# A pairwise-interaction kernel on one core: two straight blocks become turned ones, and VectorE sums three slots of a block instead of four

## The reference, cut to what matters

```
e = stack([tbl_f[ids[:, f]] for f in 0..31], axis=1)   # 1024 x 32 x 64, float32
p, q = e[:, ROW_IDX], e[:, COL_IDX]                    # the 496 pairs of 32 fields
z = einsum('bne,hne,bnh->bn', p, kernel, q)            # 1024 x 496
h = concatenate([z, dense_ctx], axis=1)                # 1024 x 512
h = maximum(h @ W_top1 + b_top1, 0)                    # 512
h = maximum(h @ W_top2 + b_top2, 0)                    # 256
y = h @ W_top3                                         # 1
```

## Time and profile before

| what | us |
|---|---|
| median of 3 runs | 391.44 (390.27 to 391.60) |
| the profiled execution, device time | 391.53 |
| its span in the profile | 389.6 |
| PE, PEld, DVE, ACT, POOL busy in it | 362.7, 281.7, 349.3, 330.6, 241.8 |

### The profile page before, as it was taken

The page is one execution under the profiler, slowest core; times in us unless marked ns, Lnnn a source line. Parts: engine busy times, 40 slices in busy tenths (PEclk is TensorE's granted clock), DMA queues, the critical chain, the costliest instruction groups (busy, mean ns, idle before and its releaser), DMA issues.

```text
span 389.6 us, 13484 instructions
## 1 busy us (share of the span) xinstructions
PE 362.7 (93%) x4800; PEld 281.7 (72%) x4800; DVE 349.3 (90%) x449; ACT 330.6 (85%) x2889; POOL 241.8 (62%) x260
## 2 busy tenths in 40 slices
PE   0467999999999999999999999999999999999996
PEld 0254757689677976799678976799668976789666
DVE  0248999999999999999999999999999999999981
ACT  1037789789998999989998999989998999989992
POOL 5677777767765776667765776767766676740000
PEclk9968899999999999999999999999999999999999
DMA  3565881111111111111111111111111111110000
GB/s 82 174 197 182 248 287 30 29 26 28 27 26 25 26 27 27 26 25 26 30 25 26 24 29 27 29 25 26 30 25 25 25 29 25 26 23 2 3 3 2
DMA packets 14563, 19.27 MB, mean 49 GB/s; under 512 B 7192, under 2 KB 7840, under 8 KB 14496
## 3 DMA queue, kind: packets, MB, share of 16 engines
q0 software_dynamic: 8192, 8.40, 10.9%
q1 hardware_dynamic: 6304, 10.00, 8.0%
HBM read 18.39 MB, written 0.00 MB: 47 GB/s over the span
## 4 chain that ended last, share of the span: by engine, by line
PE 82%; POOL 4%; ACT 4%; DMA 3%; DVE 3%; issue 3%
PE u_ps L618 28%; PE u_ps L625 26%; PE side_ps L639 13%; PE side_ps L674 5%; PE acc_ps L674 5%; POOL emb L380 4%; ACT prod_s L429 4%; DMA emb<-tbl,ids_sb 3%; PE u_ps L601 2%; DVE prod_s L534 2%; PE u_ps L705 1%; PE side_ps L698 1%; PE side_ps L666 1%; DVE prod_t L517 1%; DMA ids_sb<-ids 0%
## 5 line engine op out<-in xcount | busy, mean ns | idle before, releaser
L429 ACT ACTIVATE prod_s<-prod_s 128x64 f32<-128x64 f32 x1405 | 307.2, 327 | 43.2 <-DVE prod_s L534 43.1
L380 POOL DMA_INDIRECT emb<-tbl,ids_sb x256 | 241.6, 944 | 106.7 <-issue 44.2
L429 ACT ACTIVATION_READ_ACCUMULATOR prod_s<-prod_s 128x1 f32 x1405 | 269.2, 253 | 0.0
L534 DVE TENSOR_TENSOR prod_s<-u_ps,emb 128x1024 f32<-128x1024 f32 (+4 forms) x224 | 150.2, 718 | 10.7 <-PE u_ps L625 10.0
L517 DVE TENSOR_TENSOR prod_t<-u_ps,emb_t 128x1024 f32<-128x1024 f32 x128 | 152.8, 1213 | 4.7 <-PE u_ps L618 4.7
L618 PEld LDWEIGHTS u_ps<-emb_t,k_sb 64*128 64x128 f32 x2048 | 134.4, 192 | 21.6 <-issue 7.9
L618 PE MATMUL u_ps<-emb_t,k_sb 64*128 64x128 f32 x2048 | 140.3, 280 | 3.7 <-DVE emb_t L506 2.4
L625 PE MATMUL u_ps<-k_sb,emb_t 64*128 64x512 f32 (+5 forms) x704 | 131.5, 484 | 1.1 <-DVE emb_t L506 0.8
L625 PEld LDWEIGHTS u_ps<-k_sb,emb_t 64*128 64x128 f32 x704 | 62.8, 193 | 22.7 <-DVE prod_s L534 8.3
L639 PE MATMUL side_ps<-prod_t,pick_sb 128*32 128x256 f32 x1024 | 63.3, 382 | 0.1
L639 PEld LDWEIGHTS side_ps<-prod_t,pick_sb 128*32 128x32 f32 x1024 | 32.0, 109 | 21.4 <-issue 3.5
(11 more groups left out here) (27 smaller groups left out, 43.1 us busy)
## 6 DMA issues: line engine op xcount, KB each, us to landing
k_sb<-k_pairs SPq DMA_DIRECT2D x9, 512.0 KB, 3.7
emb<-tbl,ids_sb POOLq DMA_INDIRECT x256, 2.4
k_sb<-k_pairs SPq DMA_DIRECT2D x6, 480.0 KB, 4.5
w_sb<-w SPq DMA_DIRECT2D x1, 1024.0 KB
w_sb<-w SPq DMA_DIRECT2D x1, 512.0 KB
k_sb<-k_pairs SPq DMA_DIRECT2D x1, 448.0 KB, 4.3
h<-dense SPq DMA_DIRECT2D x8, 8.0 KB, 2.1
out<-y_row SPq DMA_DIRECT2D x8, 0.5 KB
```

The source lines that it names most:

```text
L380: nc.gpsimd.indirect_dma_start(emb[t % EMBS][:, f * EMBED:(f + 1) * EMBED], None, tables[f], bass.IndirectOffsetOnAxis(ap=ids_sb[:, t, f:f ...
L429: done = nc.scalar.activation(slot, slot, ACT.Copy, accum_out=to[:, column:column + 1])
L534: done = nc.vector.tensor_tensor(product[:, :, cols], u[:, :, cols], low, ALU.mult)
```

## The change

Blocks 6 and 23 become turned (18 turned, 14 straight). Two turned chunks have room for 16 blocks only, so the sums of the last two turned blocks go to chunk 2, 8 rows of each of its 32-row quarters; the other 24 rows of each quarter come from h0. VectorE sums 3 slots of each straight block, in 7 pairs. ScalarE's sums fall from 176 to 166 a tile. The portions of picks are 4, 4, 5 and 5 blocks, in place of four times 4, and the first portion comes after n = 22. The core of the diff:

```diff
-    order = "SSTTTSSSTSTTTSST" "TSTTSTSSSTTSSTST"
+    order = "SSTTTSTSTSTTTSST" "TSTTSTSTSTTSSTST"
-ON_DVE = 4
+ON_DVE = 3
+IN_CHUNKS = T_CHUNKS * P // (HALVES * SLOTS)      # 16
+EXTRA = NT - IN_CHUNKS                            # 2
+GAP = EXTRA * HALVES * 2                          # 8
+SHARED = QUAD - GAP                               # 24
 def sum_place(b, half, d):
-    return d % T_CHUNKS, QUAD * (half * HALVES + d // T_CHUNKS), b
+    if b < IN_CHUNKS:
+        return d % T_CHUNKS, QUAD * (half * HALVES + d // T_CHUNKS), b
+    return T_CHUNKS, QUAD * d, (b - IN_CHUNKS) * HALVES + half
-PORTIONS = 4
-PORTION = NT // PORTIONS
-LATE_SPREAD_AT, SUMS_AT, LATE_SUMS_AT, SPREAD_AT = 4, 23, 27, 31
+PORTION_AT = [0, 4, 8, 13, 18]
+PORTIONS = len(PORTION_AT) - 1
+LATE_SPREAD_AT, SUMS_AT, LATE_SUMS_AT, SPREAD_AT = 4, 22, 27, 31
 ...
+            for sums in h0:
+                nc.vector.memset(sums[:, :P].rearrange("p (q r) -> p q r", q=QUADS)[:, :, :GAP], 0.0)
 ... pick_sums, for a block past the sixteenth:
+                            for d in range(LOW):
+                                chunk, quad, place = sum_place(b, half, d)
+                                cols = slice(half * BANK + d * P, half * BANK + (d + 1) * P)
+                                done = nc.tensor.matmul(
+                                    side_ps[quad:quad + QUAD, chunk],
+                                    pick_sb[:, 30 - 2 * place:62 - 2 * place], prod_t[at % TRING][:, cols],
+                                    start=(b == IN_CHUNKS and half == 0), stop=False)
 ...
             def late_spread(t):
-                pick_sums(t, 3 * PORTION, NT)
-                spread_straight(t, side_ps[:, T_CHUNKS:]).then_inc(side_spread, 1)
+                pick_sums(t, 3)
+                spread_shared(t)
+                spread_row(t, side_ps[:, CHUNKS - 1]).then_inc(side_spread, 1)
+            def spread_shared(t):
                 pe.wait_ge(dense_loaded[t % H0S], 16 * (t // H0S + 1))
                 pe.wait_ge(summed_v, (t + 1) * NS // 2)
+                pe.wait_ge(summed_a, t * NS + S_INDEX[LAST_DIRECT] + 1)
+                return nc.tensor.matmul(side_ps[:, T_CHUNKS], h0[t % H0S][:, :P], id_sb[:], start=False, stop=True)
+            def spread_row(t, to):
                 pe.wait_ge(acc_copied, t + 1)
+                return nc.tensor.transpose(to, h0[t % H0S][:, P:], id_sb[:])
 ... the tail, on TensorE:
-            pick_sums(last, 3 * PORTION, NT)
-            spread_straight(last, spread_ps).then_inc(last_turned, 1)
+            pick_sums(last, 3)
+            spread_shared(last).then_inc(side_spread, 1)
+            spread_row(last, acc_ps[:, CHUNKS - 1]).then_inc(last_turned, 1)
```

More of the change, by code:

```diff
@@ L162, in act_slots @@
     return [s for s, _, _ in places(n)][:HALVES * BLOCKS[n].slots - ON_DVE]
[L166 to L169, removed]
+STRAIGHT = sum(HALVES * BLOCKS[n].slots for n in STRAIGHT_AT)
+CHUNKS = 4
+QUAD = 32
+QUADS = P // QUAD
 T_CHUNKS = NT * HALVES * SLOTS // P
+IN_CHUNKS = T_CHUNKS * P // (HALVES * SLOTS)
+EXTRA = NT - IN_CHUNKS
+S_CHUNKS = CHUNKS - T_CHUNKS
+PICK = T_CHUNKS * P
+GAP = EXTRA * HALVES * 2
+SHARED = QUAD - GAP
+assert T_CHUNKS == 2 and S_CHUNKS == 2 and STRAIGHT + DENSE == P + QUADS * SHARED
 DIRECT_FROM = 3
@@ L197, in w1_rows @@
 def w1_rows():
-    rows = [None] * (T_CHUNKS * P)
+    rows = [None] * (CHUNKS * P)
     for n in range(NB):
@@ L204, in w1_rows @@
                 rows[chunk * P + quad + 2 * place + s % 2] = pair_row(i, j)
[L205 to L208, removed]
+        else:
+            by_slot = {s: pair_row(i, j) for s, j, i in places(n)}
+            on_act = act_slots(n)
+            for at, s in enumerate(on_act):
+                rows[T_CHUNKS * P + ACT_COLUMN[n, at]] = by_slot[s]
+            k = S_INDEX[n]
+            for at, s in enumerate(sorted(set(by_slot) - set(on_act))):
+                rows[T_CHUNKS * P + pair_column(k // 2 * 2) + k % 2 * ON_DVE + at] = by_slot[s]
+    for i in range(DENSE):
+        rows[T_CHUNKS * P + DENSE_AT + i] = PAIRS + i
+    assert sorted(rows) == list(range(PAIRS + DENSE))
+    return rows
 K_PER_LOAD = 2
@@ L292, in build @@
         prod_t = [sb(f"prod_t{s}", [P, HALVES * BANK]) for s in range(TRING)]
-        h0 = [sb(f"h0_{t}", [P, STRAIGHT + DENSE]) for t in range(H0S)]
+        h0 = [sb(f"h0_{t}", [P, S_CHUNKS * P]) for t in range(H0S)]
         h0_t = sb("h0_t", [P, CHUNKS, P])
@@ L426, in sum_block @@
                     slot = product[:, here[at] * EMBED:(here[at] + 1) * EMBED]
-                    column = ACT_COLUMN[n] + at
+                    column = ACT_COLUMN[n, at]
                     to = h0[t % H0S] if DIRECT_FROM <= n < DIRECT_TO else acc
@@ L541, in sum_two @@
                 if (t, second) == (last, LAST_STRAIGHT):
-                    upper = buffer(t, second)[:, BANK:BANK + (ON_ACT - LAST_SHARED) * EMBED]
-                    nc.vector.tensor_reduce(h0[t % H0S][:, LAST_SHARED:ON_ACT],
+                    upper = buffer(t, second)[:, BANK:BANK + (HALVES * P - LAST_SHARED) * EMBED]
+                    nc.vector.tensor_reduce(h0[t % H0S][:, LAST_SHARED:],
                                             upper.rearrange("p (n e) -> p n e", e=EMBED), AX_X, ALU.add)
@@ L546, in sum_two @@
                 start = (t * NS + k) % SRING * HALVES * BANK + (SLOTS + BLOCKS[first].slots - ON_DVE) * EMBED
[L547 removed]
+                column = pair_column(k)
                 nc.vector.tensor_reduce(h0[t % H0S][:, column:column + 2 * ON_DVE].rearrange("p (k n) -> p k n", k=2),
@@ L628, in block_u, with pick_sums @@
                 done.then_inc(slot_filled, 1)
-            def pick_sums(t, first, stop):
-                for b in range(first, stop):
+            def pick_sums(t, portion):
+                for b in range(PORTION_AT[portion], PORTION_AT[portion + 1]):
                     at = t * NT + b
```

72 lines of the change are left out of this document (41 added, 31 removed).

## The result

The changed kernel takes 402.59 us (median of 4 runs, 401.84 to 403.40) against 391.52 us for the kernel before: the ratio is 1.029, with a 95% interval of 1.0258 to 1.0321. A second set of runs gave 1.0267 (1.0248 to 1.0286). The forecast said 395.3, range 391.4 to 399.6. The direction was right; the size was about a third of what came (3.9 of 11.1 us), and the time lies outside the range. The profiled execution took 402.99 us, its span is 401.2.

A forecast was written before the change was run, and what follows sets the result against it. PE and VectorE were taken as equally loaded, with PE's added work costing in full: +1.07 - 0.60 = +0.47 a steady tile, 3.3 over 7 tiles, plus 0.5 and 0.1, total +3.9: 395.3 us, range 391.4 to 399.6.

The forecast's parts named there:

- What PE's own work grows by: Steady tile, TensorE: two more picked blocks 0.89, two turned U blocks 0.07, transpose made a matmul 0.115; sum 1.07 us.
- Handing over, gained: Steady tile: PE's waits for VectorE shrink by 0.60 us, bounds 0 and 0.93, mostly 0.33 at blocks 2 to 4.
- The 0.93 that I started from: Steady tile of the kernel before: us that PE loses waiting for VectorE, leaving PE's own work at 43.03 of 43.96.
- Moves at no price: Steady tile: moved picks, memsets, a new ScalarE wait and later portion 3 picks and spread were claimed to cost nothing.
- The sign that I had set for an error in the picks or the handing over: New profile's steady period: 44.4 us expected; one over 44.9 would show the forecast wrong on picks or handing over.
- Tile 0: First tile, paced by VectorE and the gathers: +0.5 us, between 0 and 0.9, from picks, turned blocks and reduces.
- Tail: End of the kernel: VectorE's second reduce ends last in place of ScalarE's sums; +0.1 us, between -0.4 and +0.6.
- B: Steady tiles: no gain in handing over between PE and VectorE, +8.1, giving 399.5 us; chance 0.07.
- C: Narrow picks on TensorE run two at a time, 0.895 more a tile: 402.5 at the most, about 401; chance 0.07.
- D: Steady tiles: VectorE is the bound and PE follows; time falls by 1.54 in each of 7 tiles, to 380; chance 0.06.
- A: Steady tiles: PE floor reached, all 0.93 us of PE's waiting gained; +1.6, giving 393.0 us; chance 0.25.

The follow-up runs named there:

- The kernel with quarter reduces: Kernel before with VectorE's reduce reading one slot of each block in place of four, other three sums left out; 0.9972 on chips of 465, further sets 0.9987 and 0.9979.

## Why the prediction was wrong, step by step

- **What PE's own work grows by** (1.07): right, 1.05. Narrow picks four at a time held: 2 x 0.495 in place of 2 x 0.447, while the wide blocks beside them cost 0.44, so that the portions came out at 0.43 + 0.45. The spread was 0.16 and not 0.115; the turned blocks 0.02 and not 0.07.
- **Handing over, gained** (0.60): nearly right, 0.52. The 0.33 at n = 2 to 4 went (n = 3 and 4: -0.33), n = 19 gave 0.13, and n = 31 0.06, which I had said would stay. The 0.93 that I started from is 0.02 more than its own terms add up to (0.33 + 0.18 + 0.2 + 0.1 + 0.1).
- **"Moves at no price: the picks after n = 22 rather than 23 (hidden by VectorE's queue of filled buffers; if the cover goes, up to the 0.56 hole again on VectorE, which has slack now)"**: this is the step that failed, together with a term that I left out of the steady tile. I priced what the move does to VectorE, which can wait, and not what it does to PE, which can't: the run of blocks up to the next portion grew from four to five. And I took VectorE's reduces as 1.54 us less without asking between which blocks they now fall; for tile 0 I had counted three small ones in place of two large between blocks 13 and 23, for the steady tile nothing. The runs showed waits of 0.54 us at the end of the longer run, n = 27, and of 0.25 at n = 22, which wants the buffer of block 19, ahead of which a reduce has moved. 0.79 us in each of 7 tiles is 5.5 of the 7.3 us by which I was low. In the last tile the move of the picks costs 0.02 us in the kernel before and 0.27 in the changed one, and the wait at n = 27 is there only where the moved picks meet the moved reduce; no price for either alone would have found it. VectorE's hole did grow, from 0.56 to 1.19, as foreseen, and that was no comfort: idle time behind picks is slack that the run after it lacks. The sign that I had set for an error in the picks or the handing over, a period above 44.9, came.
- **Tile 0** (+0.5): +1.46. The wait at n = 27 is there too: the traces of the changed kernel have it in all 8 tiles (0.27 us of PE's idle time each), those of the kernel before in none. The rest of tile 0 was not taken apart, and the head's 0.38 is unexplained.
- **Tail** (+0.1): +0.5. I let VectorE's reduce end last. The narrow picks end at the same moment, and the chain goes through them, then one copy of three chunks.
- **The sum**: 0.53 of the 1.32 us a tile is what the forecast had (0.47), 0.79 the waits of the failed step.
- **The rivals.** B gave 399.5 with no gain in handing over, 3.1 us short: the gain was there, and a new loss ate more than it. C's 402.5 is the measured time, but its mechanism is refuted (0.495, not 0.895, a block). D and A are refuted by the period, which grew by more than PE's own work did while VectorE got lighter. No case of mine had the mechanism that decided.
- **What stays open.** The changed kernel with its picks after n = 23, and the kernel before with its picks after n = 22, were never run on the chip of 391.8. What the move costs, 0.02 and 0.27, is read in the last tile only; for the other tiles, and for the time of the whole kernel (8 x 0.27 = 2.2 us by an estimate from that tile), it is not shown. That the reduce holds back block 27 is read from VectorE's order and from the two kernels that have only one of the two moves; no run put the reduce alone back in its place.

## What to carry to other kernels

Between two engines of equal load and few buffers, it is not enough to add up what each has to do: the order decides who waits. The side work of the producer is breathing space for the consumer, and the side work of the consumer (here a reduce of 0.46 us) holds back every buffer behind it. Before calling a moved portion free, write down both orders for the run of blocks around it and see, block by block against the buffers, what stands ahead of the buffer that the producer wants next; do the same for side work that moves by itself because a count has changed. And a time that agrees with a rival does not confirm it: here C gave 402.5, and a single timeline row refuted it.

## What the runs showed of the hardware that was not expected

The same kernel takes 391 us on one chip and 465 us on two others, each within 1% of its median, with a granted clock of 0.95 to 0.99 in the traces of the slower chips and 0.98 to 1.00 in the others. The kernel with quarter reduces, which differs from the kernel before by 0.2% there, is the nearest to a trace of it on such a chip. First and fourth section of its page:

```profile
PE 393.7 (85%) x4800; PEld 295.3 (64%) x4800; DVE 328.1 (71%) x452; ACT 335.3 (73%) x2889; POOL 242.0 (52%) x260
...
PE 71%; DVE 11%; issue 10%; ACT 4%; another core or an unknown queue 3%; DMA 1%; POOL 0%; DVEq 0%
```

PE's busy share is 85% where the earlier trace rows has 93%, and "issue", time in which an engine waited for nothing that the profile shows, is 10% of the chain. In one of its tiles PE's starts lie 0.5 to 1.3 us apart at 13 places, where the kernel before on the other chip has 4, and a steady tile is about 52.5 us. Idle time of PE without a releaser, in pieces above 0.25 us, is seen in the steady tiles of all fourteen traces of these chips and in those of none of the others, and in every one of the fourteen its last piece lies 5 to 9 us ahead of the last gather of embeddings; the 48 us and more after it have none. What holds PE's instructions up was not found, and that it has to do with the gathers is a guess from this coincidence. It means that a verdict on such a chip about PE's own instructions does not carry over to the other kind.
